# Marked neighbours turned by transposing transfers instead of TensorE, in a LoRA, cross-attention and graph-network kernel

## The chip, the cores and the metric

The kernel runs on one NeuronCore of a Trainium2 chip. The metric is the device time of one execution in microseconds, the median over runs. Below, TensorE is PE in the profile's lines, VectorE is DVE, ScalarE is ACT, GpSimd is POOL, SyncE is SP. SP computes nothing here; it waits for semaphores and issues DMA transfers, one after the other, in its own order.

## The reference

Four batches (b = 0 to 3) of 256 rows of 512 numbers pass through four layers. The context has 4 x 64 rows of 512.

```
x   = x + 0.5 * sum_n softmax(x @ router_W.T + router_b)[n] * (a_sum @ lora_B[n].T)   # 8 experts, rank 64
      # a_sum = x times the sum of the context's rows taken as lora_A; then nan_to_num
Q,K,V = x@Wq.T+bq, ctx@Wk.T+bk, ctx@Wv.T+bv         # 32 heads of 16, 64 keys with a mask
x   = layernorm(x + softmax(Q K.T / 4) V @ Wo.T + bo) * g + b
for layer in (L2, L3):                              # two graph layers, the same weights
    idx = the 8 nearest of 512 points by ctx (64 coordinates)       # per batch
    for i in range(4):
        p = leaky_relu(x)
        x = x + (W[i] @ p + sum over the 8 neighbours of W[i] @ p[neighbour]) / 9
```

As the weights of centre and neighbour are the same, the sum is a product with a 512x512 matrix per batch: the 0/1 matrix of neighbours, turned so that the contracted index lies on the partitions, plus the identity. That matrix is what this change is about.

## The kernel before, in words

The work is cut into steps named by kind, batch and part, as dist1_3. Five texts (PE_STEPS, ACT_STEPS, DVE_STEPS, POOL_STEPS, SP_STEPS, lines 47 to 123) list the steps of each engine in the order in which it runs them; a number behind a colon is the PSUM bank (PE) or the buffer (DVE) used. An engine works strictly in its order; each step first waits for the semaphores of what it reads and of what still reads the place it writes. A step of TensorE that takes a bank waits until the bank's former content has been read (wait_read, line 575). The orders come out of a search outside the kernel; nothing of its costs stands in the code. Products are made of two float32r parts (hi, lo) in three passes.

Steps that this text speaks of:

- Loads: SP issues all first loads before its step list, in the order xyz0, ctxT, x0, loraB, wk, xyz1, x1, small, wq, wv (with bv and mask_col), wo (with g_all and b_all) (line 490). ld_x2, ld_xyz2 and so on come later.
- lora, router (PE), low, rE (ACT), rA, rB (DVE): the router's softmax, and mix, the rows weighted for each expert. mixed (PE) turns them, mh and ml make hi and lo. ua, ub, uc (PE, 24 + 12 + 12 products) are the update; raw and nan (DVE) make x1 of it. xh, xl split x1; qa, qb, qc (PE, 24 + 12 + 12 products) are the queries; qh, qf (ACT), ql (POOL) keep them as q_hi and q_lo.
- keys and values (PE), kh, kl, vr. kst writes the keys to DRAM, ks (six transfers) brings them back as k_stack. qsh (eight transfers) and qs (four) bring q_hi and q_lo into q_stack, sd (two) the shifts. sc (PE) gives scores for the maxima (mx), shift turns these, w (PE) is the stacked product that the softmax reads, at and norm attend, rows and oa, ob, oc are the output product, st, ce, ln the layer norm.
- dist (PE, line 676) gives the distances of 128 points to all 512 in one bank. near (DVE, line 1157) takes the 8 greatest (max) and writes the tile with these replaced by -2^127 into near_of[:, i] in bf16. There is one near_of for all batches, so near of batch b waits until batch b-1 has been turned.
- adjT (PE, line 677): when all four near of a batch are there, 16 transposes of 128x128 bf16 with ident_h turn near_of into two PSUM banks. adjC (ACT, line 867) makes the 0/1 matrix adj[:, b] of it in one 128x2048 instruction, reading PSUM. diag (POOL, line 1095) adds the identity. adj[:, 2] and adj[:, 3] hold att_hi and wo_hi before, so adjC2 and adjC3 wait for the last oc.
- Graph layers: units b, i = 0 to 7. wa, wb, wc, wd (PE) multiply with W, uh, ul split, ga, gb, gc, gd (PE) multiply with adj[:, b], pt (DVE) adds to points, lk (DVE), ph (ACT), pl (POOL) make the next p. The units of batch 0 start while the attention of later batches still runs.

points[:, b] is used for other things early: it holds the coordinates of batch 1, the bias bv (until vr), and x_bo[b], the input turned with bo added (ACT, xb, line 899).

The step that the change takes off TensorE:

```python
for m in range(KC):
    for n in range(KC):
        last = pe.transpose(dst[:, m * H + n * P:m * H + (n + 1) * P],
                            near_of[:, n, m * P:(m + 1) * P], ident_h[:])
last.then_inc(turned_done, 1)
```

## Time and profile before

| | |
|---|---|
| median of 3 runs | 377.6 us (377.03 to 379.24) |
| the profiled execution | 378.0 us from its first to its last instruction |
| TensorE busy | 367.6 us, 97% |
| VectorE busy | 272.0 us, 72% |
| ScalarE busy | 177.0 us, 47% |
| GpSimd busy | 129.0 us, 34% |
| mean granted TensorE clock | 0.995 |

The profile is of one execution. An engine's busy time counts its instructions, not its waits or its issues of transfers. For TensorE, matmuls overlap each other by modelled ends, so differences between starts tell its pace. The last instruction of a transfer's issue (SPq) is the time that SP is held by it; the landing comes later. "The chain" is followed back from the last instruction to what released each.

### The profile page before, as it was taken

What the parts mean: (1) busy time and instruction counts of PE and PEld (TensorE: products, weight loads), DVE (VectorE), ACT (ScalarE), POOL (GpSimd) and SP (SyncE); (2) the same over time, 40 slices, a digit from 0 to 9 for tenths busy, and PEclk for the clock granted to TensorE, in tenths of its full rate; (3) what the DMA queues carried; (4) which work ended last, traced back from release to release, by engine and by line L of the source; (5) the groups of instructions that cost most, each with busy time, mean ns of one, the idle gap of its engine ahead of it and who ended that gap; (6) DMA issues with size and microseconds to landing.
All of it is one profiled execution on the core that took longest, in us unless ns stands there. A gap on an engine that the chain in (4) does not pass through costs nothing.

```text
span 378.0 us, 6569 instructions
## 1 busy us (share of the span) xinstructions
PE 367.6 (97%) x2396; PEld 311.0 (82%) x2396; DVE 272.0 (72%) x427; ACT 177.0 (47%) x308; POOL 129.0 (34%) x125
## 2 busy tenths in 40 slices
...
GB/s 201 317 348 159 24 55 155 78 9 178 34 20 232 105 0 116 102 0 3 0 3 2 0 0 2 0 2 1 2 0 2 0 2 0 3 0 2 0 85 139
DMA packets 25056, 22.47 MB, mean 59 GB/s; under 512 B 9537, under 2 KB 20546, under 8 KB 25026
## 3 DMA queue, kind: packets, MB, share of 16 engines
...
q10 hardware_dynamic: 674, 0.02, 0.1%
...
## 4 chain that ended last, share of the span: by engine, by line
PE 85%; DVE 4%; ACT 4%; DMA 3%; issue 2%; SPq 1%; DVEq 0%; ACTq 0%
PE slot L564 82%; DMA wk<-in_WkT 3%; ACT k_blk_hi L943 2%; PE slot L684 1%; PE slot L693 1%; SPq L448 1%; PE slot L725 1%; ACT probT L976 1%; DVE p_full L1321 1%; DVE points L1331 1%; ACT adj L874 1%; DVE inv_full L1267 0%; ACT L976 0%; DVE stats L1282 0%; DVE shift L1255 0%
## 5 line engine op out<-in xcount | busy, mean ns | idle before, releaser
L1065 POOL TENSOR_TENSOR p_lo<-p_full,p_hi 128x512 fp32r<-128x512 f32 x64 | 86.0, 1362 | 157.1 <-ACT p_hi L1016 157.0
L1026 ACT ACTIVATE u_hi<-slot 128x512 fp32r<-128x512 f32 x64 | 36.2, 593 | 69.3 <-PE slot L564 69.0
L1326 DVE TENSOR_TENSOR u_lo<-slot,u_hi 128x512 fp32r<-128x512 f32 x64 | 42.4, 684 | 31.5 <-ACT u_hi L1026 31.5
L1016 ACT ACTIVATE p_hi<-p_full 128x512 fp32r<-128x512 f32 x64 | 39.0, 627 | 55.3 <-DVE p_full L1321 55.3
L564 PE MATMUL slot<-adj,u_hi 128*128 128x512 f32 x256 | 64.8, 392 | 0.1
L564 PE MATMUL slot<-fs_hi,p_hi 128*128 128x256 f32 x256 | 64.8, 286 | 0.0
L1331 DVE SCALAR_TENSOR_TENSOR points<-slot,points 128x512 f32<-128x512 f32 x64 | 42.7, 684 | 30.4 <-PE slot L564 30.4
L564 PE MATMUL slot<-adj,u_lo 128*128 128x512 f32 x256 | 64.1, 391 | 0.0
L564 PE MATMUL slot<-fs_lo,p_hi 128*128 128x256 f32 x256 | 64.1, 283 | 0.0
L1321 DVE SCALAR_TENSOR_TENSOR p_full<-points 128x512 f32<-128x512 f32 x64 | 54.3, 863 | 8.9 <-POOL p_lo L1065 6.3
L564 PEld LDWEIGHTS slot<-adj,u_lo 128*128 128x128 f32 x256 | 47.5, 188 | 10.1 <-issue 0.4
L564 PEld LDWEIGHTS slot<-adj,u_hi 128*128 128x128 f32 x256 | 46.4, 188 | 8.8 <-DVE u_lo L1326 0.3
L564 PEld LDWEIGHTS slot<-fs_hi,p_hi 128*128 128x128 f32 x256 | 48.9, 191 | 1.6 <-issue 0.7
L564 PEld LDWEIGHTS slot<-fs_lo,p_hi 128*128 128x128 f32 x256 | 49.0, 191 | 0.9 <-issue 0.2
L564 PE MATMUL slot<-fs_hi,p_lo 128*128 128x256 f32 x256 | 42.9, 285 | 0.1
L564 PEld LDWEIGHTS slot<-fs_hi,p_lo 128*128 128x128 f32 x256 | 36.6, 191 | 1.8 <-issue 0.8
L1065 POOL TENSOR_TENSOR q_lo<-q_full,q_hi 128x512 fp32r<-128x512 f32 x8 | 10.7, 1348 | 46.5 <-ACT q_full L930 46.5
L976 ACT ACTIVATE probT<-slot,mask_col 128x1024 f32<-128x1024 f32 x16 | 17.7, 1116 | 16.2 <-PE slot L564 16.0
L1255 DVE TENSOR_REDUCE shift<-slot 128x16 f32<-128x1024 f32 x16 | 19.4, 1218 | 1.5 <-PE slot L564 1.5
L943 ACT ACTIVATE k_blk_hi<-kT_hi,half_col 32x256 fp32r<-32x256 f32 x32 | 14.4, 497 | 0.9 <-PE slot L564 0.5
L564 PE MATMUL slot<-xyz_n,xyz 128*128 128x512 f32 x24 | 13.9, 685 | 0.3 <-issue 0.3
L564 PE MATMUL slot<-mixT_hi,loraB_hi 128*128 128x256 f32 x64 | 13.7, 296 | 0.0
...
## 6 DMA issues: line engine op xcount, KB each, us to landing
q_stack<-q_hi SPq DMA_DIRECT2D x32, 128.0 KB, 2.5
x_in<-in_xT SPq DMA_DIRECT2D x8, 256.0 KB, 4.2
q_stack<-q_lo SPq DMA_DIRECT2D x16, 128.0 KB, 2.4
out_points<-points SPq DMA_DIRECT2D x8, 256.0 KB, 2.0
...
```

Of the source, the lines that this page charges most:

```text
L448: sp.dma_start(dst, src).then_inc(loads[name], 16)
L564: return pe.matmul(dst, lhsT, rhs, start=start, stop=stop, skip_group_check=True)
L684: last = pe.transpose(dst[:, m * H + n * P:m * H + (n + 1) * P], near_of[:, n, m * P:(m + 1) * P], ident_h[:])
L943: act.activation(k_blk_hi[rows, :, 2 * j + a, :], kT_hi[rows, :, b * V:(b + 1) * V].bitcast(F32), ACT.Copy, scale=half_col[rows, a:a + 1]) ...
L976: act.activation(probT[:, i % 2, :], both_banks("w", b, i)[:], ACT.Exp, bias=mask_col[:, b:b + 1], scale=QK_SCALE).then_inc(prob_ready, 1)
L1016: act.activation(p_hi[b][:, (i % 2) * H:(i % 2 + 1) * H], p_full[:, p_buf[b, i]], ACT.Copy)\
L1026: act.activation(half_of(u_hi[:, u], i % 2), bank("wa", b, i // 2, i % 2), ACT.Copy)\
L1065: pool.tensor_tensor(lo[:, cut], full[:, cut], hi[:, cut].bitcast(F32), ALU.subtract)\
L1255: dve.tensor_reduce(pairs, both_banks("sc", b, i)[:].rearrange("p (j a v) -> p j a v", a=2, v=V), AX_X, ALU.max, negate=True).then_inc(max ...
L1321: dve.scalar_tensor_tensor(p_full[:, p_buf[b, i]], pts, SLOPE, pts, ALU.mult, ALU.max)\
L1326: dve.tensor_tensor(half_of(u_lo[:, u], i % 2), bank("wa", b, i // 2, i % 2), half_of(u_hi[:, u], i % 2).bitcast(F32), ALU.subtract).then_ ...
L1331: dve.scalar_tensor_tensor(pts, bank("ga", b, i // 2, i % 2), 1.0 / (TOPK + 1), pts, ALU.mult, ALU.add).then_inc(points_ready, 1)
```

## The change

Each of the four near of a batch is followed by its own transfer nt (SP): a transposing DMA that writes near_of[:, i], 128x512 in bf16, turned into nearT[b][:, :, i*128:(i+1)*128] in SBUF. Sixteen of them take the place of the four adjT with their 64 transposes. nearT lies in points[:, 0] for batch 0, in points[:, 2] for batch 1 (nt1 waits until vr has read bv there), and for batches 2 and 3 in near_late, which lies where q_stack lies (nt2 and nt3 wait for the last w). near of batch b waits for all four transfers of batch b-1, adjC for those of b. adjC reads nearT in place of PSUM. xb0 waits for adjC0 and xb2 for adjC1, as they write the same places. ident_h and its two instructions on POOL go. All five orders are new; kst stands later in SP's, behind qsh0.

In the diff, the texts of the orders are cut to their first lines.

```diff
 PE_STEPS = """
-mb0:0 dist0_0:7 dist0_1:5 lora0:6 dist0_2:2 dist0_3:4 router0:0 keys:6,7 lora1:2 mixed0:0,1 router1:2 values:4,5
-mixed1:2,0 dist1_0:7 adjT0:4,5 ua0:3,6 ub0 uc0 dist1_1:4 dist1_2:5 ua1:1,2 qa0:7,3 qb0 dist1_3:6 ub1 sc0_0:4,5 qc0
-uc1 sc0_1:0,1 lora2:6 adjT1:2,3 router2:0 dist2_0:1 sc0_2:4,5 sc0_3:6,7 qa1:3,2 dist2_1:7 qb1 dist2_2:4 shift0:5
-dist2_3:1 lora3:6 mixed2:0,3 router3:5 sc1_0:6,7 qc1 ua2:0,4 w0_0:2,3 sc1_1:6,7 ub2 sc1_2:2,3 w0_1:6,7 uc2 w0_2:2,3
-w0_3:6,7 at0_0:0,1,5 at0_1 at0_2 at0_3 sc1_3:6,7 qa2:3,2 qb2 shift1:0 mixed3:6,7 norm0:4,5 qc2 sc2_0:0,1 rows0:5,4
...
+dist0_0:4 dist0_2:7 lora0:3 router0:1 dist0_1:5 dist0_3:0 mixed0:6,4 mb0:2 lora1:1 dist1_0:0 dist1_1:3 dist1_2:1
+ua0:6,5 ub0 router1:2 uc0 keys:6,7 dist1_3:4 mixed1:0,5 values:2,3 qa0:1,4 qb0 ua1:6,0 sc0_2:2,3 ub1 qc0 uc1 lora2:7
+sc0_0:0,1 qa1:6,5 router2:7 sc0_1:2,3 sc0_3:0,1 qb1 qc1 mixed2:7,2 dist2_1:3 shift0:4 ua2:0,1 sc1_2:2,3 sc1_0:4,5
+ub2 sc1_1:2,3 w0_1:6,7 w0_0:4,5 lora3:0 uc2 w0_2:6,7 at0_0:2,3,0 at0_1 w0_3:4,5 router3:1 sc1_3:6,7 at0_2 at0_3
+shift1:5 dist2_2:6 qa2:4,7 qb2 mixed3:3,5 norm0:0,1 dist2_0:2 qc2 ua3:6,1 sc2_2:4,5 sc2_0:2,3 ub3 uc3 dist2_3:7
+w1_1:4,5 rows0:0,1 w1_0:2,3 oa0 w1_2:2,3 at1_0:6,7,4 at1_1 ob0 w1_3:2,3 oc0 at1_2 at1_3 sc2_1:2,3 qa3:0,1 norm1:4,5
+sc2_3:6,7 qb3 rows1:4,3 qc3 oa1 ob1 shift2:2 oc1 wa0_0:7,6,1 sc3_1:0,1 wb0_0 wc0_0 sc3_2:4,5 sc3_0:2,3 wd0_0
+ga0_0:0,1 w2_0:4,5 gb0_0 gc0_0 w2_1:6,7 w2_2:4,5 at2_0:2,3,0 at2_1 w2_3:6,7 gd0_0 at2_2 at2_3 wa0_1:4,1,1 wb0_1
+wc0_1 rows2:5,3 norm2:6,7 wa1_0:0,2,0 wd0_1 wb1_0 wc1_0 wd1_0 sc3_3:6,7 oa2 shift3:6 ob2 ga1_0:6,7 oc2 gb1_0
...
 ACT_STEPS = """
-sq0 low0 rE0 lbh wqh low1 mh0_0 rE1 mh0_1 kh kb0 sq1 woh mh1_0 adjC0 xh0_0 mh1_1 xh0_1 sq2 qh0_0 xb0_0 qf0_0 qh0_1
-xb0_1 qf0_1 xh1_0 low2 adjC1 xh1_1 rE2 kb1 qh1_0 sh0 qf1_0 xb1_1 low3 mh2_0 mh2_1 vb0 qh1_1 qf1_1 rE3 xb1_0 ex0_0
...
+sq0 low0 rE0 lbh mh0_0 sq1 mh0_1 low1 adjC0 rE1 wqh xh0_0 kh kb0 xh0_1 mh1_0 mh1_1 xb0_1 woh qf0_0 xb0_0 qh0_0 sq2
+qh0_1 qf0_1 xh1_0 vb0 low2 xb1_0 xh1_1 rE2 kb1 mh2_0 qf1_0 sh0 qf1_1 mh2_1 qh1_0 qh1_1 adjC1 ex0_0 ex0_1 xb1_1 low3
+ex0_2 ex0_3 xh2_0 xh2_1 rE3 sh1 kb2 ac0_0 ac0_1 vb1 qf2_0 mh3_1 mh3_0 qh2_0 ah0_1 xb2_1 xb2_0 qh2_1 ah0_0 qf2_1
...
 DVE_STEPS = """
-mr fa a_ready fm init near0_0 rA0 near0_1 near0_3 near0_2 rB0 rA1 mk ml0_0 rB1 kl vr ml0_1 near1_0 ml1_0 raw0_0
-nan0_0 raw0_1 xl0_0 nan0_1 ml1_1 xl0_1 near1_1 near1_2 near1_3 raw1_0 mx0_0 nan1_0 raw1_1 mx0_1 xl1_0 nan1_1 rA2
-mx0_3 xl1_1 mx0_2 near2_0 rB2 near2_1 sl0 near2_2 ml2_0 mx1_0 ml2_1 rA3 near2_3 rB3 mx1_1 raw2_0 mx1_2 nan2_0 raw2_1
...
+a_ready near0_0 near0_2 rA0 rB0 mr near0_3 init near0_1 ml0_0 fa ml0_1 fm raw0_0 near1_0 near1_1 rA1 raw0_1 nan0_0
+rB1 near1_2 kl nan0_1 xl0_0 near1_3 xl0_1 vr ml1_0 ml1_1 mx0_2 mk raw1_0 nan1_0 raw1_1 xl1_0 nan1_1 mx0_0 xl1_1 rA2
+mx0_1 rB2 mx0_3 ml2_0 near2_1 sl0 ml2_1 mx1_2 mx1_0 raw2_0 mx1_1 nan2_0 raw2_1 nan2_1 mx1_3 rA3 xl2_0 xl2_1 rB3 sl1
+rc0 near2_2 dv0_1 ml3_0 dv0_0 ml3_1 near2_0 al0_0 mx2_0 mx2_2 raw3_1 al0_1 raw3_0 near2_3 nan3_0 nan3_1 xl3_1 st0_0
...
 POOL_STEPS = """
-zb wql lbl zk wol ql0_0 ql0_1 zr ql1_0 ql1_1 ql2_0 ql2_1 diag0 diag1 pl0_0 pl0_1 ql3_0 ql3_1 pl1_1 pl1_0 pl0_2 pl0_3
...
+lbl zb zr wql zk ql0_0 ql0_1 wol ql1_1 ql1_0 ql2_1 ql2_0 pl0_0 diag0 pl0_1 pl0_2 diag1 ql3_1 pl0_3 ql3_0 pl1_0 pl1_1
...
 SP_STEPS = """
-kst ld_xyz2 ks0 ld_x2 qsh0 qs0 ld_x3 sd0 qsh1 qs1 ks1 sd1 ld_fs qsh2 qs2 sd2 ks2 ld_xyz3 qsh3 sd3 ks3 qs3
+nt0_1 nt0_0 nt0_2 nt0_3 ld_xyz2 nt1_2 nt1_3 ld_x2 qsh0 kst nt1_0 nt1_1 qs0 ks0 sd0 ld_x3 qsh1 sd1 qs1 ks1 ld_fs ks2
+qsh2 qs2 sd2 ld_xyz3 qsh3 ks3 qs3 sd3 nt2_3 nt2_2 nt2_0 nt2_1 nt3_0 nt3_2 nt3_1 nt3_3
 """
@@ -152,7 +153,7 @@
             banks_of[kind, b, i] = where
             read_before[kind, b, i] = list(dict.fromkeys(holder[k] for k in where if k in holder))
         for part, k in enumerate(where):
-            holder[k] = (kind, b, i, 0 if kind in ("keys", "values", "adjT", "sc", "w") else part)
+            holder[k] = (kind, b, i, 0 if kind in ("keys", "values", "sc", "w") else part)
     for kind, b, i, where in dve_steps:
         if kind == "lk":
             p_buf[b, i], p_holder[b, i] = where[0], holder.get(("p", where[0]))
@@ -174,7 +175,6 @@
         points = sb("points", [P, B, ST, H])
         adj = sb("adj", [P, B, KC, H], F32R)
         ident = sb("ident", [P, P])
-        ident_h = sb("ident_h", [P, P], BF16)
         xyz_0 = sb("xyz", [P, H])
         xyz_n0 = sb("xyz_n", [P, H])
         near_of = sb("near_of", [P, KC, H], BF16)
@@ -194,6 +194,7 @@
         v_rows = sb("v_rows", [P, B // 2, H])
         v_blk = sb("v_blk", [P, NH // 2, PART])
         wk, wv = under(("wk", [P, KC, H], F32), ("wv", [P, KC, H], F32))
+        near_late, = under(("near_late", [P, 4, H], F32))
         q_stack = sb("q_stack", [P, NH // 2, S], F32R)
         ctx_t, = under(("ctx_t", [P, KC, B * V], F32))
         attT, = under(("attT", [P, KC, S], F32))
@@ -240,6 +241,9 @@
         x_bo = [points[:, b].rearrange("p t h -> p (t h)").rearrange("p (c s) -> p c s", c=KC) for b in range(B)]
+        nearT = [place.rearrange("p a n -> p (a n)").bitcast(BF16)[:, 0:KC * H].rearrange("p (m n) -> p m n", m=KC)
+                 for place in (points[:, 0], points[:, 2], near_late[:, 0:2], near_late[:, 2:4])]
+
         front = ExitStack()
         def fb(name, shape, dt=F32):
@@ -523,6 +527,14 @@
                             row = PART * part + HD * a
                             src = k_bounce[which].rearrange("c (j a d) b v -> b a d (c j) v", a=2, d=HD)[b, a]
                             sp.dma_start(k_stack[row:row + HD, :, a, :].bitcast(F32), src).then_inc(k_stacked, 16)
+                elif kind == "nt":
+
+                    if b == 1:
+                        sp.wait_ge(v_ready, 1)
+                    if b >= 2:
+                        after(sp, weights_done, "w", B - 1, KC - 1)
+                    after(sp, near_ready, "near", b, i)
+                    sp.dma_start_transpose(nearT[b][:, :, i * P:(i + 1) * P], near_of[:, i]).then_inc(turned_done, 16)
                 elif kind == "qsh":
                     after(sp, q_hi_ready, "qh", b, 0, each=2)
                     after(sp, q_hi_ready, "qh", b, 1, each=2)
@@ -593,8 +605,6 @@
                     pe.wait_ge(ctx_filled, 1)
                 elif kind == "dist":
                     after(pe, near_ready, "near", b, i)
-                elif kind == "adjT":
-                    after(pe, adj_copied, "adjC", b)
                 elif kind == "sc":
                     after(pe, max_ready, "mx", b, i)
                 elif kind == "shift":
@@ -674,16 +684,6 @@
                     after(pe, sq_ready, "sq", b)
                     pe.wait_ge(dve_consts, 2)
                     mm(bank("dist", b, i), xyz[b][:, i * P:(i + 1) * P], xyz_n[b], True, True).then_inc(dist_done, 1)
-                elif kind == "adjT":
-                    pe.wait_ge(idents, 2)
-                    for n in range(KC):
-                        after(pe, near_ready, "near", b, n)
-                    dst = both_banks("adjT", b)[:].bitcast(BF16)
-                    for m in range(KC):
-                        for n in range(KC):
-                            last = pe.transpose(dst[:, m * H + n * P:m * H + (n + 1) * P],
-                                                near_of[:, n, m * P:(m + 1) * P], ident_h[:])
-                    last.then_inc(turned_done, 1)
                 elif kind == "mixed":
                     after(pe, mix_ready, "rB", b, each=ST)
                     cols = cols_of("mixed", b)
@@ -868,11 +868,11 @@
                     if b >= 2:
                         after(act, output_done, "oc", B - 1)
-                    after(act, turned_done, "adjT", b)
+                    act.wait_ge(turned_done, 16 * KC * (b + 1))
                     act.wait_ge(dve_consts, 3)
                     act.activation(adj[:, b].rearrange("p m n -> p (m n)"),
-                                   both_banks("adjT", b)[:].bitcast(BF16), ACT.Relu,
+                                   nearT[b].rearrange("p m n -> p (m n)"), ACT.Relu,
                                    bias=taken_bias[:], scale=TAKEN_SCALE).then_inc(adj_copied, 1)
                 elif kind == "low":
                     if b >= 1:
@@ -900,10 +900,12 @@
                     loaded(act, "bo_col")
                     after(act, x1_ready, "nan", b, i)
+                    if b == 0:
+                        after(act, adj_copied, "adjC", 0)
                     if b == 1:
                         after(act, dist_done, "dist", 1, 3)
                     if b == 2:
-                        act.wait_ge(v_ready, 1)
+                        after(act, adj_copied, "adjC", 1)
                     for c in (2 * i, 2 * i + 1):
                         act.activation(x_bo[b][:, c], x1[:, c, :], ACT.Identity, bias=bo_col[:, c:c + 1])\
                            .then_inc(x_bo_ready, 1)
@@ -1033,9 +1035,6 @@
             link(pool.memset(ident[:], 0.0))
             pool.affine_select(out=ident[:], in_=ident[:], compare_op=ALU.not_equal, fill=1.0, base=0,
                                pattern=[[-1, P]], channel_multiplier=1).then_inc(idents, 1)
-            link(pool.memset(ident_h[:], 0.0))
-            pool.affine_select(out=ident_h[:], in_=ident_h[:], compare_op=ALU.not_equal, fill=1.0, base=0,
-                               pattern=[[-1, P]], channel_multiplier=1).then_inc(idents, 1)
             link(pool.memset(diag[:], 1.0))
             link(pool.affine_select(out=diag[:], in_=diag[:], compare_op=ALU.is_ge, fill=0.0, base=0,
@@ -1055,7 +1054,7 @@
                     last = pool.memset(cols[:, :, 2 * c + half], 1.0)
             last.then_inc(blk_consts, 1)
             pool.wait_ge(blk_consts, 2)
-            pool.wait_ge(idents, 2)
+            pool.wait_ge(idents, 1)
             def low_part(lo, full, hi, parts, ready):
@@ -1158,7 +1157,7 @@
                     after(dve, dist_done, "dist", b, i)
                     if b >= 1:
-                        after(dve, turned_done, "adjT", b - 1)
+                        dve.wait_ge(turned_done, 16 * KC * b)
                     tile = bank("dist", b, i)
                     link(dve.max(top8[:, i], tile))
                     dve.match_replace(near_of[:, i], top8[:, i], tile, TAKEN).then_inc(near_ready, 1)
```

## Rows read from the trace of the kernel before

**Rows 1.** The page: its span, busy times, and the chain's shares
```profile
span 378.0 us, 6569 instructions
...
PE 367.6 (97%) x2396; PEld 311.0 (82%) x2396; DVE 272.0 (72%) x427; ACT 177.0 (47%) x308; POOL 129.0 (34%) x125
...
PE 85%; DVE 4%; ACT 4%; DMA 3%; issue 2%; SPq 1%; DVEq 0%; ACTq 0%
```

**Rows 2.** Windows: from:to, length, busy us by engine, granted clock, DMA share, GB/s
```profile
37.00:375.00 338.00, 334.94 (x2275) 289.80 (x2274) 250.37 (x379) 160.95 (x282) 111.65 (x90) 1.00 0.14 36
...
15.90:20.20 4.30, 4.30 (x13) 3.55 (x14) 3.98 (x10) 0.53 (x1) 0.00 (x0) 0.65 1.10 335
```

**Rows 3.** Chain in order of time: start, us, what
```profile
4.29 11.36 DMA wk<-in_WkT
...
36.15 0.89 PE slot L684 x16
...
59.58 0.91 PE slot L684 x16
...
175.80 0.91 PE slot L684 x16
...
219.75 0.91 PE slot L684 x16
```

**Rows 4.** Timeline, ScalarE: start, us, instruction, idle time before
```profile
40.50 1.97 ACT L874 ACTIVATE adj<-slot,taken_bias 128x2048 fp32r<-128x2048 bf16 x1
...
201.12 1.98 ACT L874 ACTIVATE adj<-slot,taken_bias 128x2048 fp32r<-128x2048 bf16 x1 [4.17 <-PE slot L564]
```

**Rows 5.** Timeline of SP: its issues
```profile
12.37 2.82 SPq L448 DMA_DIRECT2D wv<-in_WvT  x1
...
19.48 0.43 SPq L448 DMA_DIRECT2D b_all<-in_ln_b  x1
...
35.26 0.83 SPq L525 DMA_DIRECT2D k_stack<-k_hi_bounce  x2
...
56.96 5.29 SPq L496 DMA_DIRECT2D q_stack<-q_hi  x8
...
89.41 2.52 SPq L496 DMA_DIRECT2D q_stack<-q_lo  x4
```

**Rows 6.** DMA issues: KB each, us from issue to landing
```profile
q_stack<-q_hi SPq DMA_DIRECT2D x32, 128.0 KB, 2.5
...
b_all<-in_ln_b SPq DMA_DIRECT2D x1, 256.0 KB, 9.0
```

**Rows 7.** Timeline, VectorE: steps near0, nan0_0 and the following raw0_1
```profile
15.42 0.69 DVE L1163 MAX8 top<-slot 128x8 f32<-128x512 f32 x1
...
16.82 0.69 DVE L1163 MAX8 top<-slot 128x8 f32<-128x512 f32 x1
...
42.17 0.43 DVE L1237 TENSOR_SCALAR scratch<-x_in 128x512 f32<-128x512 f32 x1
...
44.44 0.68 DVE L1225 SCALAR_TENSOR_TENSOR x_in<-slot,x_in 128x512 f32<-128x512 f32 x1
```

**Rows 8.** Timeline, TensorE: keys, values, mixed1, dist1_0, transposes, two products of the update
```profile
15.89 8.83 PE L564 MATMUL slot<-ctx_m,wk 128*128 128x256 f32 x32 [2.43 <-DMA wk<-in_WkT]
...
27.32 7.10 PE L564 MATMUL slot<-wv,ctx_t 128*128 128x512 f32 x16
34.26 1.04 PE L693 MATMUL slot<-ident,mix 128*128 128x128 f32 x8
35.13 1.02 PE L564 MATMUL slot<-points 128*128 128x512 f32 x2
35.99 1.06 PE L684 MATMUL slot<-ident_h,near_of 128*128 128x128 bf16 x16
...
37.17 0.40 PE L564 MATMUL slot<-mixT_hi,loraB_lo 128*128 128x256 f32 x2
37.41 0.40 PE L564 MATMUL slot<-mixT_lo,loraB_hi 128*128 128x256 f32 x2
```

More of the change, by code:

```diff
@@ new lines @@
+w3_0:0,1 gc1_0 w3_1:2,3 gd1_0 ga0_1:4,0 w3_2:2,3 at3_0:6,7,1 at3_1 gb0_1 w3_3:2,3 gc0_1 gd0_1 at3_2 at3_3 dist3_2:2
+wa1_1:5,3,1 wb1_1 wc1_1 dist3_0:6 norm3:0,1 wd1_1 wa0_2:4,7,0 ga1_1:0,2 gb1_1 dist3_1:1 gc1_1 gd1_1 wb0_2 wc0_2
+dist3_3:2 wd0_2 rows3:5,3 oa3 ob3 oc3 ga0_2:4,7 gb0_2 gc0_2 wa2_0:0,2,0 wb2_0 wa1_2:3,5,1 wc2_0 gd0_2 wd2_0 wb1_2
+ga2_0:7,1 gb2_0 wc1_2 wd1_2 gc2_0 gd2_0 ga1_2:6,4 wa3_0:2,0,0 wb3_0 gb1_2 wc3_0 gc1_2 gd1_2 wd3_0 wa0_3:6,7,1 wb0_3
+wc0_3 ga3_0:4,5 wd0_3 gb3_0 wa1_3:1,0,0 gc3_0 gd3_0 wb1_3 wc1_3 wd1_3 ga0_3:5,6 ga1_3:4,3 gb1_3 wa3_1:2,7,0 gc1_3
```

93 lines of the change are left out of this document (41 added, 52 removed).

## The prediction

> **What bounds the kernel now.** I read the page first: TensorE is busy 97% of a span of 378.0 us, the next engine (VectorE) 72%, and the chain that ended last runs 85% through TensorE [rows 1]. The windows say the same by stage: from 37 to 375 us TensorE is busy 334.94 of 338.00 us, so it sits idle 3.06 us in all, at a granted clock of 1.00 [rows 2]. In that stretch a microsecond of TensorE work taken out is a microsecond gained, and one added wait of TensorE is one lost. The chain in order of time then shows what the removed step costs: the four groups of 16 transposes (L684) stand on it with 0.89, 0.91, 0.91 and 0.91 us, and before all of them the chain hangs on the load of wk, which lands at 15.65 us [rows 3]. So there are two regimes: before about 16 us the loads set the pace, after it TensorE does.
>
> The profiled execution took 378.0 us, 0.4 us more than the median of the three timed runs (377.6). The sum is made against 378.0, and 0.4 us is taken off at the end. A measurement of this kernel can tell about 0.5% (1.9 us) from no change.
>
> **Removed.** The 64 transposes: 0.89 + 3 x 0.91 = 3.62 us of the chain [rows 3]. TensorE's PSUM banks 4,5 and 2,3 are no longer held by them; what that gives is left to the new orders. POOL loses one memset and one select of ident_h before 2.2 us, with 16 us idle before its next work: nothing. ScalarE's adjC reads SBUF in place of PSUM; it takes 1.97 us for 128x2048 [rows 4], the shape stays, and a few tenths more or less would be hidden on an engine that is busy half of the span: nothing.
>
> **Added.** Sixteen transposing transfers of 128 KB, SBUF to SBUF, all issued by SP. The trace has none. What I need is how long SP is held by one (i), and when the first four have landed (T). From below: a plain 128 KB transfer q_stack<-q_hi holds SP 5.29/8 = 0.66 us and lands 2.5 us after its issue [rows 5, 6]. From above: the longest time any issue held SP is 2.82 us (wv) [rows 5]. It can't be below nothing, since SP has no such transfer now. I take i between 0.7 and 1.0 us, near the row of the same size and the same memories, and keep 2.8 us for the range.
>
> The Trainium skill speaks on both sides here. *Advanced Engine Details and Errata*, section X-Bar Transpose (TRN2), says that transposing DMAs are as fast as regular ones; by it i is the lower bound and the sum stays as below. *VectorE: DVE Perf Modes*, section The three transpose paths, gives 1309 ns for one 128x128 bf16 transpose by DMA against 390 ns on TensorE; if four of them in a transfer simply add up, i is an estimated 5.2 us, and the change ends near 393 us. On TensorE's side that page does not fit this case: 16 transposes take 0.91 us in the stream here, 57 ns each [rows 3].
>
> **First set (b = 0), the place that I think decides.** near0 needs until about 18.5 us (two of its steps of 1.40 us each [rows 7] stand behind rB0, which can't start before x0 has been through lora0 and router0), but SP is issuing the initial loads until 19.48 + 0.43 = 19.9 us, and its queue is full: b_all, issued at 19.48, lands 9.0 us later, at 28.5 us [rows 5, 6]. Packets of the SP queue land in order, so nt0 comes behind b_all: 28.5 us plus 0.5 MB at the 380 GB/s the queue then reaches, 1.4 us: T = 29.9 us.
>
> In DVE's new order near1_0 comes right after raw0_0, and it now waits for all four of nt0 (near_of is single). Behind it on DVE queue near1_0 and near1_1 (1.40 us each, from start to start), rA1 (0.3 us), raw0_1 (0.7) with nan0_0 (from the start of nan to the next raw 2.3) and rB1 (1.8) [rows 7]. On ScalarE adjC0 waits for the same four, with rE1, wqh and xh0_0 behind it; adjC0's 1.97 us lie beside the two near steps, so rE1 is in time for rB1. TensorE's mixed1 needs rB1: it can start at M = T + 8.0 = 37.9 us.
>
> When would TensorE be there by itself? x1 lands about 2.1 us after wk (0.75 MB), near 18 us. From there the new order has half of lora1 (0.9), dist1_0 to dist1_2 (2.6), 48 products of the update at 0.12 us (5.8), router1 (0.1), the keys (6.9: 8.7 us from start to start now, of which the low clock takes 1.5 to 1.8) and dist1_3 (0.9): 35.2 us [rows 8]. So mixed1 waits about 2.7 us. Against before: at 35.99 us, where the first transposes start, TensorE has done the values (6.9) and mixed1 (0.9), which the new order has still before it, while at M the new one has done three more dist (2.6) and the 48 update products (5.8) [rows 8]. That is 0.5 us more, so the orders are even for M = 36.5 us. With M = 37.9 the new one is 1.4 us behind. After M the values (6.9 us) cover near1_2, kl, nan0_1, xl0_0 and near1_3 (7.4 us with mixed1's 0.9 in front), and wq_lo is ready at T + 10.6: nothing more is lost.
>
> **The clock.** From 15.9 to 20.2 us the granted clock is 0.65 on average, after TensorE had sat idle from 13.5 to 15.9 us [rows 2, 8]; at 1.00 the same work would take 1.5 us less. The new order has idle time just before 18 us too (only mixed0 and mb0 are left until x1 is there), so I count the same loss in both, and keep 1.5 us to either side for the range.
>
> **Second set (b = 1).** nt1_2 and nt1_3 wait for v_ready (about 47 us) and stand ahead of ld_x2; lora2 comes at 57.6 us (the first product of the queries at M + 7.8 = 45.7, then 96 products of 0.12 us and one score step, 11.9 us in all), and x2 needs 3 us plus 2i: hidden up to i = 3. On SP then: 8 issues of q_hi (5.3 us from 57.1 us on, when q_hi is whole), kst (0.8), nt1_0 and nt1_1 (2i), 4 of q_lo (2.5), 6 of k_stack (2.8), 2 of shiftT (1.4, at q_hi's rate), and 2.5 us to the last landing: 72.4 + 2i [rows 5, 6]. TensorE reaches w0_1 after 84 more products (10.1), six score steps (2.8) and 3.8 us of lora2, mixed2, dist2_1, shift0 and router2, at 57.6 + 16.7 = 74.3 us. It is covered up to i = 0.95, all but the end of my interval; above it TensorE loses 2 us for each us of i. I take 0.
>
> **Third and fourth (b = 2, 3).** nt2 waits for the last scores' product w3_3 (170 us now), adjC2 ran at 201 us [rows 4]; near3 waits for nt2, and adjC3 ran some 20 us later. SP has nothing else to do there. Even 4 x 2.8 + 2.5 = 14 us is hidden: nothing.
>
> **The orders.** Everything else is the same work in another order. With 3.06 us idle left in 37 to 375 us [rows 2] it can't win more than that there; I count 0, with up to 2 us either way.
>
> **Sum.** 378.0 - 3.62 + 1.4 = 375.8 us; less 0.4: 375.4 us.
>
> **Rivals.** (A) *The front is not late.* For it: the wait on DVE hangs on a queue whose rate I estimated, and a T of 28.5 would give M = 36.5 (loss 0). With 1 to 2 us of the 3.06 idle us recovered it gives 372 to 374 us. Against: nt0 can hardly land before b_all.
> (B) *The gain is absorbed.* nt0 lands 2 to 3 us later than I think (a transposing packet that takes twice as long as a plain one puts T at 31.3), or i is 1.5 us, which costs 1 us at w0: 377.3 to 380 us.
> (C) *The transfers hold SP, and it is slower.* One mechanism: i. With i = 2.8 the last of nt0 is issued at 31.1 and lands at 33.6, M = 41.6, a loss of 5.1 us in place of 1.4; before w0_1 another 2 x (2.8 - 0.95) = 3.7 us. Total 375.4 + 3.7 + 3.7 = 382.8 us. For it: k_stack's transfers of 64 KB hold SP 0.42 us, b_all's of 256 KB 0.43 and q_hi's of 128 KB 0.66 [rows 5], so the issue cost goes by the form and not by the bytes, and a transpose is a new form; wv's issue shows how long one can be held. The turning point: with T = 19.9 + 4i + 2.5, the loss (4i - 6.1) + 2(i - 0.95) exceeds 3.62 from i = 1.9 us on.
> (D) *The change doesn't do what it says:* TensorE's work shrinks by 3.6 us, but it idles as much more in the order as searched. It would give 378 us and is counted with B.
>
> **Numbers.** Forecast 0.40 (374 to 377.3), A 0.20 (371 to 374), B with D 0.17 (377.3 to 380), C 0.23 (380 and up, open end). The range 371.5 to 381 leaves out 0.02 of A and 0.18 of C. Faster by over 0.5% means below 375.7: A (0.20) and 0.28 of the forecast's 0.40, in sum 0.48. Slower means above 379.5: C and 0.02 of B, 0.25. The same: 0.27.
>
> **What would show it.** No L684 in the new trace and TensorE's busy time lower by about 3.6 us. On SP, sixteen new issues with their length: under 1 us for the forecast, over 1.9 for C. On DVE, an idle gap before a near1 step at 28 to 30 us released by the DMA of nearT, and on TensorE a gap of 2 to 3 us before the transposes of mixed1 (none for A, over 6 us for C). No gap before the first q_stack,k_stack product. It would be wrong if nt0 lands ahead of the loads issued before it, if transposing transfers slow the other transfers, or if the new order opens gaps elsewhere in 45 to 375 us that have nothing to do with the transfers.

## The result, and the profile after

The changed kernel takes 391.0 us (389.54 to 392.31, 4 runs) against 377.4 us before (377.6 in the table ahead, with one run fewer); the ratio is 1.035 (95% interval 1.0318 to 1.0389). It is slower by 13.6 us, outside the range of the prediction and on the other side of its forecast. The profiled execution took 389.54 us, its span 387.7 us.

First the page of the kernel after, the lines that answer to [rows 1]:

```profile
span 387.7 us, 6449 instructions
...
PE 367.5 (95%) x2332; PEld 307.1 (79%) x2332; DVE 277.0 (71%) x427; ACT 172.4 (44%) x304; POOL 130.8 (34%) x123
...
PE 70%; DVE 15%; SPq 6%; issue 4%; ACT 2%; DMA 1%; POOL 1%; DVEq 0%; ACTq 0%; POOLq 0%
```

The transposes are gone, yet TensorE is as busy as before (367.5 against 367.6 us), and it is idle for 387.7 - 367.5 = 20.2 us against 378.0 - 367.6 = 10.4. So two things have to be found: about 10 us of new idle time, and what filled up the 3.6 us that were taken out. The chain says where to look: VectorE has 15% of it in place of 4%, and SP's issues 6% in place of 1% [rows 1].

Windows of the kernel after (columns as in [rows 2]): the stretch of [rows 2], then three short ones around the largest stall.

```profile
37.00:375.00 338.00, 326.44 (x2157) 277.27 (x2156) 249.55 (x370) 160.21 (x288) 116.62 (x86) 0.99 0.18 41
```

```profile
66.30:69.90 3.60, 0.19 (x2) 0.02 (x1) 3.57 (x4) 0.63 (x1) 1.83 (x2) 0.94 1.01 314
69.90:72.90 3.00, 3.00 (x12) 2.81 (x13) 2.90 (x8) 2.13 (x6) 0.00 (x0) 0.51 0.74 158
72.90:76.00 3.10, 3.10 (x26) 2.86 (x26) 1.84 (x4) 2.53 (x7) 0.00 (x0) 1.00 0.74 165
```

From 37 to 375 us TensorE is now idle 11.56 us in place of 3.06. Behind the stall at 66 us it runs at a granted clock of 0.51, the level of 1.2 GHz, for some 3 us: pairs of 128x256 matmuls start 0.43 us apart there (from 71.32 us on) and 0.24 us apart right after (from 72.95 us on). This is TensorE's timeline at the new waits (in brackets: idle time before, and what ended it):

```profile
39.37 1.06 PE L693 MATMUL slot<-ident,mix 128*128 128x128 f32 x8 [1.65 <-DVE mix L1213]
48.06 0.48 PE L576 MATMUL slot<-x_hi,wq_hi 128*128 128x256 f32 x2 [0.77 <-DVE near_of L1163]
...
69.88 1.22 PE L576 MATMUL slot<-k_blk_hi,q_hi 128*128 128x512 f32 x2 [3.41 <-DVE shift L1254]
...
151.43 0.36 PE L576 MATMUL slot<-fs_hi,p_hi 128*128 128x256 f32 x1 [1.39 <-issue]
```

The first is the wait for nt0 that the prediction worked out. The largest has no transfer in it. VectorE and GpSimd of the kernel after, in front of it (the steps nan1_1 and mx0_0, and wol):

```profile
62.38 1.51 DVE L1236 TENSOR_SCALAR scratch<-x_in 128x512 f32<-128x512 f32 x1
63.92 1.67 DVE L1237 SCALAR_TENSOR_TENSOR x<-x_in,scratch 128x512 f32<-128x512 f32 x1
65.62 1.39 DVE L1238 TENSOR_SCALAR scratch<-x_in 128x512 uint32<-128x512 f32 x1
67.05 1.67 DVE L1239 COPY_PREDICATED x<-scratch,x_in 128x512 f32<-128x512 uint32 x1
68.62 1.21 DVE L1254 TENSOR_REDUCE shift<-slot 128x16 f32<-128x1024 f32 x1
```

```profile
61.87 6.26 POOL L1064 TENSOR_TENSOR wo_lo<-wo_raw,adj 128x512 fp32r<-128x512 f32 x4
```

The same step nan1_1 in the kernel before, its first two instructions:

```profile
60.43 0.58 DVE L1237 TENSOR_SCALAR scratch<-x_in 128x512 f32<-128x512 f32 x1
61.04 0.69 DVE L1238 SCALAR_TENSOR_TENSOR x<-x_in,scratch 128x512 f32<-128x512 f32 x1
```

These four instructions of nan1_1 took 0.58, 0.69, 0.45 and 0.75 us before (the first of nan0_0 took 0.43 [rows 7]). Here they take 6.2 us in sum instead of 2.5, and for nearly all that time GpSimd does wol, which the new order puts there. The reduction that TensorE waits for (L1254) is queued behind them.

SP of the kernel after; L537 is the transposing transfer:

```profile
19.24 8.50 SPq L537 DMA_TRANSPOSE points<-near_of  x4
...
49.72 2.50 SPq L537 DMA_TRANSPOSE points<-near_of  x2
52.31 1.51 SPq L452 DMA_DIRECT2D x_in<-in_xT  x2
...
66.63 3.75 SPq L537 DMA_TRANSPOSE points<-near_of  x2
```

One transfer holds SP 2.1 us while its queue is full of loads, 1.25 us with little else in flight and 1.9 us behind the q_hi transfers; single ones took 1.19 to 2.64. The forecast took 0.7 to 1.0. The table of DMA issues has them from issue to landing (median us), early and late ones:

```profile
points<-near_of SPq DMA_TRANSPOSE x8, 4.9
near_late<-near_of SPq DMA_TRANSPOSE x8, 2.5
```

### The profile page after: what moved, and what is told of

Same layout as the page of the kernel before. It is cut to its first block, busy times and chain, and to the rows that moved or that the text cites. A ratio compares the mean times of both kernels' runs of the same rounds, so it can differ in the third digit from the quotient of the medians.

```text
span 387.7 us, 6449 instructions
## 1 busy us (share of the span) xinstructions
PE 367.5 (95%) x2332; PEld 307.1 (79%) x2332; DVE 277.0 (71%) x427; ACT 172.4 (44%) x304; POOL 130.8 (34%) x123
## 4 chain that ended last, share of the span: by engine, by line
PE 70%; DVE 15%; SPq 6%; issue 4%; ACT 2%; DMA 1%; POOL 1%; DVEq 0%; ACTq 0%; POOLq 0%
PE slot L576 68%; SPq L452 4%; DVE p_full L1320 2%; DVE points L1301 2%; SPq L537 2%; DVE points L1330 2%; DMA points<-near_of 1%; DVE near_of L1163 1%; DVE top L1162 1%; DVE x L1237 1%; DVE scratch L1238 1%; ACT k_blk_hi L945 1%; DVE u_lo L1325 1%; DVE scratch L1236 1%; PE slot L693 1%
## 5 line engine op out<-in xcount | busy, mean ns | idle before, releaser
L576 PE MATMUL slot<-adj,u_hi 128*128 128x512 f32 x256 | 65.9, 394 | 2.2 <-ACT u_hi L1028 1.6
L576 PE MATMUL slot<-adj,u_lo 128*128 128x512 f32 x256 | 66.6, 394 | 0.9 <-DVE u_lo L1325 0.9
L576 PEld LDWEIGHTS slot<-adj,u_lo 128*128 128x128 f32 x256 | 46.3, 188 | 10.1 <-DVE u_lo L1325 1.5
L576 PE MATMUL slot<-fs_hi,p_lo 128*128 128x256 f32 x256 | 43.9, 285 | 0.3 <-ACT p_hi L1018 0.3
L576 PEld LDWEIGHTS slot<-fs_hi,p_lo 128*128 128x128 f32 x256 | 38.2, 191 | 3.9 <-issue 1.0
L1254 DVE TENSOR_REDUCE shift<-slot 128x16 f32<-128x1024 f32 x16 | 19.4, 1220 | 8.2 <-PE slot L576 8.2
L576 PE MATMUL slot<-x_hi,wq_hi 128*128 128x256 f32 x64 | 14.3, 307 | 1.0 <-DVE near_of L1163 0.8
L945 ACT ACTIVATE k_blk_hi<-kT_hi,half_col 32x256 fp32r<-32x256 f32 x32 | 14.4, 497 | 0.4
```

Source lines behind the costliest of these rows:

```text
L576: return pe.matmul(dst, lhsT, rhs, start=start, stop=stop, skip_group_check=True)
L945: act.activation(k_blk_hi[rows, :, 2 * j + a, :], kT_hi[rows, :, b * V:(b + 1) * V].bitcast(F32), ACT.Copy, scale=half_col[rows, a:a + 1]) ...
L1254: dve.tensor_reduce(pairs, both_banks("sc", b, i)[:].rearrange("p (j a v) -> p j a v", a=2, v=V), AX_X, ALU.max, negate=True).then_inc(max ...
```

## Experiments

All are built from the kernel after. "Theory O" in the expectations is that the new orders make the loss, "theory T" that the transfers do. Medians are of runs taken beside runs of the kernel before (377.2 to 377.8 us each time).

### The two halves of the change, apart

e1_old_orders: the five orders of before, without adjT, with the 16 transfers in SP's. From the kernel after it differs in the orders alone.

```diff
 PE_STEPS, ACT_STEPS, DVE_STEPS, POOL_STEPS: those of before, without adjT0 to adjT3
 SP_STEPS
-kst ld_xyz2 ks0 ld_x2 qsh0 qs0 ...
+nt0_0 nt0_1 nt0_3 nt0_2 kst ld_xyz2 ks0 nt1_0 ld_x2 nt1_1 nt1_2 nt1_3 qsh0 qs0 ...
```

> The five orders of before, with adjT taken out and the sixteen transfers put into SP's order (nt0 first, nt1 around ld_x2 and ahead of qsh0, nt2 and nt3 last). If the loss comes from the new orders (theory O), this is faster than before by the 3.6 us of the transposes: 373 to 375 us. If it comes from the transfers themselves (theory T: SP held, VectorE waiting for landings, packets in the way of others), it is slower than before: 380 us or more.

Measured: 377.3 us (10 runs), ratio 0.9988 (0.9963 to 1.0014): the whole loss is gone, but the gain of 3.6 us that theory O expected isn't there either. Its page:

```profile
span 373.9 us, 6454 instructions
...
PE 362.9 (97%) x2332; PEld 306.8 (82%) x2332; DVE 272.4 (73%) x427; ACT 177.2 (47%) x308; POOL 127.7 (34%) x123
```

e7_no_transfers: the new orders without any transfer (near writes where adjC reads), with adjC1 right behind sq2. An earlier form, e2_no_transfers, had left adjC1 in its place, and near2_1 waited for it.

```diff
-                    sp.dma_start_transpose(nearT[b][:, :, i * P:(i + 1) * P], near_of[:, i])...
-                    act.wait_ge(turned_done, 16 * KC * (b + 1))
+                    after(act, near_ready, "near", b, 0) ... 3
-dve.match_replace(near_of[:, i], ...)
+dve.match_replace(near_at[b][:, i], ...)
```

> The new orders with no transfers at all: near writes the marked tile where adjC reads it, unturned, so the neighbours' matrix is left unturned (that part of the computation is left out). Theory O: little is won, 2 to 4 us, as the wait before mixed1 (1.8 us) goes: 386 to 389 us. Theory T: the whole loss goes, 378 us or less.

> The new orders with no transfers, as in the kernel without transfers above, and adjC1 moved to behind sq2 on ScalarE, so that near2_1 no longer waits for it (an artefact of that kernel, 5 us; the turning is left out again). Theory O: 386 to 388 us, as most of the loss has nothing to do with the transfers. Theory T: 380 us or less.

Measured: e2 394.0 us (1.0399 to 1.0493), e7 388.2 us, ratio 1.027 (1.0247 to 1.0298). Both leave the matrix of neighbours unturned. TensorE and GpSimd of e7_no_transfers have the largest stall of the kernel after, at the same step and of the same length, without any transfer:

```profile
65.91 1.22 PE L576 MATMUL slot<-k_blk_hi,q_hi 128*128 128x512 f32 x2 [3.42 <-DVE shift L1256]
...
57.90 6.26 POOL L1065 TENSOR_TENSOR wo_lo<-wo_raw,adj 128x512 fp32r<-128x512 f32 x4
```

e4_plain_copy kept the transfers as plain copies (again unturned; each row of a partition goes in four pieces of 256 bytes):

```diff
-sp.dma_start_transpose(nearT[b][:, :, i * P:(i + 1) * P], near_of[:, i])
+sp.dma_start(nearT[b][:, :, i * P:(i + 1) * P], near_of[:, i].rearrange("p (m n) -> p m n", m=KC))
```

> The changed kernel with each transposing transfer made a plain copy of the same 128 KB between the same places (the turning is left out). Theory T with the form of the transfer as its cause: issues fall from 1.2 to 2.6 us to 0.6 us each and 5 us or more are won. Theory O: the wait before mixed1 shrinks by 1 to 2 us and little else, 388 to 390 us.

Measured: 391.3 us (1.0315 to 1.0425). With SP's queue full at 20 us four plain copies hold it 6.90 us; four transposing ones 8.50. For the last two batches, with nothing else in flight, one plain copy holds it 0.60 us in the median, one transposing transfer 1.22.

What follows: the transfers in the old orders are as fast as the transposes. With the same transfers the new orders are 391.0 - 377.3 = 13.7 us slower than the old ones. With neither transfers nor transposes they are still 10.8 us slower than the kernel before, which has 3.6 us of transposes more to do. In the change the transfers account for 391.0 - 388.2 = 2.8 us; the rest is the orders. e8_old_tuned put dist2_0 ahead of router2 on TensorE in e1, where it waited 0.62 us:

> The old orders with the transfers and dist2_0 ahead of router2 on TensorE. The transposes used to fill the time in which ScalarE makes low2 (a gap of 0.8 us at 56 us with the transfers); dist2_0 fills it now: 0.5 to 0.8 us faster than the old orders with the transfers, 376.5 us, and 1 us faster than before. If removed work is given back elsewhere: the same as before.

Measured: 377.1 us (12 runs, 0.9966 to 1.0013), no difference, where 1 us had been expected.

### The waits of the new orders, one by one

e3_wol_early moves wol on GpSimd, away from nan1_1 (the expectation calls the step nan1_0).

```diff
-lbl zb zr wql zk ql0_0 ql0_1 wol ql1_1 ...
+lbl zb zr wql zk wol ql0_0 ql0_1 ql1_1 ...
```

> The changed kernel with one step moved: GpSimd's wol before ql0_0, so that its four subtractions no longer run beside VectorE's nan1_0. Theory O in its sharpest form (GpSimd's tensor_tensor doubles the time of VectorE's steps out of SBUF, and TensorE waits 3.6 us for the maxima queued behind): 3 to 4 us faster than the changed kernel, 387 to 388 us. Theory T: no change, 391 us.

Measured: 393.6 us (1.039 to 1.047). The four instructions were back at 0.42, 0.69, 0.43 and 0.76 us and TensorE's wait was gone, but nothing was won: the median is 2.6 us above the kernel after. The next row of TensorE's timeline in e3_wol_early shows why:

```profile
82.50 1.77 PE L576 MATMUL slot<-q_stack,k_stack 100*128 100x256 f32 x7 [4.14 <-DMA q_stack<-shiftT]
```

A second wait, for q_stack at w0, ran beside the first and had been hidden by it; alone it is 0.7 us longer than the first was. The other 2 us of the difference are not explained. On SP, nt1_0 and nt1_1 (3.77 us), q_lo and k_stack stood ahead of shiftT. This is the wait that the prediction priced at 2(i - 0.95), and I had overlooked it when I wrote the expectation. e5_sp_early adds an SP order with both earlier; e6_front_too adds four small moves before 60 us.

```diff
 SP_STEPS
-nt0_1 nt0_0 nt0_2 nt0_3 ld_xyz2 nt1_2 nt1_3 ld_x2 qsh0 kst nt1_0 nt1_1 qs0 ks0 sd0 ...
+nt0_1 nt0_0 nt0_2 nt0_3 ld_xyz2 kst ks0 nt1_0 nt1_1 nt1_2 nt1_3 ld_x2 qsh0 qs0 sd0 ...
```

> The changed kernel with wol before ql0_0 on GpSimd, and SP's order changed: kst and ks0 right after ld_xyz2, and all four nt1 ahead of ld_x2. Theory O (two delays lay side by side, VectorE beside GpSimd's wol and SP's queue before w0_1, so that taking away the first alone showed the second): both stalls near 66 to 82 us go, 4 to 5 us, and the stretch at half clock after them, 1.7 us: 385 us. If the losses of this stretch have another cause, it stays at 390 to 394 us.

> The kernel before this one with three more steps moved: mb0 and mr back to the front of TensorE's and VectorE's orders, near1_3 right behind near1_2, and xl0_0 ahead of nan0_1. Theory O: mb0 costs 1 us less (it fills the wait for the coordinates) and the 0.9 us wait before the first queries goes: 1.5 to 2 us faster than with SP's order alone. No change if those waits are hidden by the landing of nt0.

Measured: e5 387.2 us (1.022 to 1.0282), 2 us above what was expected, e6 386.7 us (1.0203 to 1.026), no clear difference from e5 where 1.5 to 2 us were expected. Now mixed1 was the largest wait, as VectorE's and TensorE's timelines of e5_sp_early show:

```profile
32.08 0.70 DVE L1162 MAX8 top<-slot 128x8 f32<-128x512 f32 x1 [5.25 <-DMA points<-near_of]
```

```profile
39.98 1.51 PE L693 MATMUL slot<-ident,mix 128*128 128x128 f32 x8 [4.51 <-DVE mix L1213]
```

VectorE stands still for 5.25 us with rA1 and rB1 queued behind near1_0. e11_router_first puts them ahead:

```diff
 ACT_STEPS
-low1 adjC0 rE1 wqh
+low1 rE1 adjC0 wqh
 DVE_STEPS
-raw0_0 near1_0 near1_1 rA1 raw0_1 nan0_0 rB1 near1_2
+raw0_0 rA1 raw0_1 nan0_0 rB1 near1_0 near1_1 near1_2
```

> e5_sp_early with rA1, raw0_1, nan0_0 and rB1 ahead of near1_0 on VectorE (near1_0 waits for the landing of nt0, and mixed1 of TensorE hung on rB1 behind it), and rE1 ahead of adjC0 on ScalarE. Theory E: TensorE's wait of 4.7 us at 35 us goes, and the stretch of 3.41 us at half clock behind it (1.7 us): 387.2 - 6.4 = 381 us (380 to 383). Rival (the wait covers another one close behind it, as in e3_wol_early): a wait for near1 or the values' consumers takes its place and it stays above 385 us.

Measured: 385.0 us (1.0145 to 1.0244). The wait at 35 us went, but only 2.2 us of the 6.4 came out; TensorE then waited 1.58 us for near1_3, and a slow clock stretch appeared at 146.7 us. e13_pool_early takes GpSimd away from VectorE in that late stretch:

```diff
-pl0_0 diag0 pl0_1 pl0_2 diag1 ql3_1 pl0_3 ql3_0
+pl0_0 diag0 pl0_1 diag1 ql3_1 pl0_2 pl0_3 ql3_0
```

> e11_router_first with diag1 and ql3_1 of GpSimd (adj<-adj,ident and q_lo<-q_full,q_hi) moved ahead of pl0_2, into its idle time from 131.5 to 139.1 us. In e11_router_first they ran at 140.35 and 142.05 us beside VectorE's points<-points,rstd,b_all (2.48 us for two, elsewhere 1.42) and p_full<-points (3.27 us for two, elsewhere 1.28), and TensorE then waited 1.6 us for p_hi, with a stretch of 3.41 us at half clock behind it (1.7 us). Theory C (VectorE is slowed by GpSimd's tensor_tensor beside it, and that makes the wait): p_full goes back to 1.3 to 2 us, the wait of 1.6 us goes, 385.0 - 3.3 = 381.7 us (381 to 383.5). Rival (the slow VectorE instructions have another reason, or the wait is ScalarE's): p_full stays at 3.27 us wherever GpSimd is, and the time within 1 us of 385.0.

VectorE and GpSimd of e11_router_first, then of e13_pool_early, at the same steps:

```profile
138.46 2.48 DVE L1301 SCALAR_TENSOR_TENSOR points<-points,rstd,b_all 128x512 f32<-128x512 f32 x2
141.05 3.27 DVE L1320 SCALAR_TENSOR_TENSOR p_full<-points 128x512 f32<-128x512 f32 x2
...
139.11 1.28 POOL L1064 TENSOR_TENSOR p_lo<-p_full,p_hi 128x512 fp32r<-128x512 f32 x1 [7.59 <-ACT p_hi L1018]
140.35 1.74 POOL L1097 TENSOR_TENSOR adj<-adj,ident 128x512 fp32r<-128x512 f32 x1
142.05 1.72 POOL L1064 TENSOR_TENSOR q_lo<-q_full,q_hi 128x512 fp32r<-128x512 f32 x1
```

```profile
140.20 2.47 DVE L1301 SCALAR_TENSOR_TENSOR points<-points,rstd,b_all 128x512 f32<-128x512 f32 x2
142.78 1.29 DVE L1320 SCALAR_TENSOR_TENSOR p_full<-points 128x512 f32<-128x512 f32 x2
...
140.84 1.28 POOL L1064 TENSOR_TENSOR p_lo<-p_full,p_hi 128x512 fp32r<-128x512 f32 x1 [5.06 <-ACT p_hi L1018]
```

Measured: 382.9 us (1.0085 to 1.017), 2.1 us less; the runs of the two kernels don't overlap (382.0 to 383.2 against 383.6 to 386.0). The same two p_full take 1.29 us instead of 3.27 once GpSimd is idle beside them, while points<-points,rstd,b_all, which still has p_lo beside it, stays at 2.47. GpSimd's own instructions got shorter too (1.74 and 1.72 us back to 1.31 and 1.30). That VectorE and GpSimd slow each other is shown by this pair, and by e3_wol_early. The windows of the same stretch (e11_router_first, then e13_pool_early) show that the low clock went with the wait:

```profile
146.80:150.00 3.20, 3.20 (x17) 3.20 (x17) 2.47 (x3) 2.42 (x6) 3.12 (x3) 0.50 0.63 143
```

```profile
146.80:150.00 3.20, 3.03 (x26) 2.69 (x26) 2.38 (x4) 2.17 (x5) 3.12 (x3) 1.00 0.80 184
```

e14_front_too then moves three steps:

```diff
 PE_STEPS: mb0 ahead of dist0_0
 DVE_STEPS: mr ahead of a_ready, near1_3 right behind near1_2
```

> e13_pool_early with near1_3 right behind near1_2 and mr ahead of a_ready on VectorE, and mb0 ahead of dist0_0 on TensorE. Theory E (single waits in the order, each worth its own length once nothing lies beside it): TensorE's wait of 1.74 us at 43.9 us for near1_3 goes, and up to 1 us before 10 us: 1.7 to 2.7 us below e13_pool_early, 379.5 us (378.5 to 381). Rival (each wait that is taken away is replaced by the next): no more than 0.7 us below e13_pool_early.

Measured: 380.4 us (1.0049 to 1.0096), 2.5 us less. The same three moves were in e6_front_too, where TensorE still waited 4.55 us for mixed1 and they gave no clear gain.

### SP's queue once more

e15_two_more moves two more steps, and e16_x2_first mends what it broke:

```diff
 e15_two_more, against e14_front_too
-DVE: near1_3 kl nan0_1 xl0_0 xl0_1 vr       ACT: dev3 ph3_0 uh2_0 uh2_1
+DVE: near1_3 nan0_1 xl0_0 xl0_1 kl vr       ACT: dev3 uh2_0 uh2_1 ph3_0
 e16_x2_first, against e15_two_more
-SP:  ld_xyz2 kst ks0 nt1_0 nt1_1 nt1_2 nt1_3 ld_x2 qsh0
+SP:  ld_xyz2 ld_x2 kst ks0 nt1_0 nt1_1 nt1_2 nt1_3 qsh0
```

> e14_front_too with two steps moved: kl of VectorE behind xl0_1, and ph3_0 of ScalarE behind uh2_1. In e14_front_too TensorE waits 1.78 us at 42.7 us for x_lo (kl, 1.65 us, runs on VectorE ahead of nan0_1), and 1.57 us at 199.4 us for u_hi, which on ScalarE is queued behind ph3_0 (it waits 5.98 us for a p_full that VectorE gives late, after 3.39 us for points<-points,rstd,b_all beside GpSimd). Theory E (each wait was put there by the order and is worth its own length): both go, 380.4 - 1.5 - 1.6 = 377.3 us (376.5 to 378.5), as before. Rival (the two waits hide others of the same length): over 379 us.

> e15_two_more with ld_x2 ahead of kst on SP and nothing else. In e15_two_more the later kl held up kst (46.46 us), and ks0 and the four transposing transfers nt1 (5.12 us of SP from 52.85 us on) stood ahead of ld_x2, which was issued at 58.07 us; TensorE waited 4.78 us for it (until 61.49 us), with a stretch of 3.41 us at half clock behind it. Theory S (SP's queue made that wait): it goes, 386.8 - 4.8 - 1.7 = 380.3 us (379 to 381). Rival (another wait stands behind it, for q_stack or the shifts at w0): over 382.5 us.

Measured: e15 386.8 us (1.0225 to 1.0279), 9 us over the expectation; e16 379.9 us (1.0035 to 1.0081). SP and TensorE of e15_two_more, then SP of e16_x2_first:

```profile
46.46 0.38 SPq L515 DMA_DIRECT2D k_lo_bounce<-kT_lo  x1
...
52.85 5.12 SPq L536 DMA_TRANSPOSE points<-near_of  x4
58.07 1.04 SPq L451 DMA_DIRECT2D x_in<-in_xT  x2
```

```profile
61.49 3.48 PE L575 MATMUL slot<-x_in,points 128*72 128x256 f32 x8 [4.78 <-DMA x_in<-in_xT]
```

```profile
42.62 0.91 SPq L451 DMA_DIRECT2D x_in<-in_xT  x2
...
53.04 5.13 SPq L536 DMA_TRANSPOSE points<-near_of  x4
```

A VectorE step, kl, put 7.3 us later (44.78 us in place of 37.46) held up the store of the keys, which held up k_stack and four transposing transfers, which held up a load that had nothing to do with them. With the load in front, 6.8 us came back. Of e15's own two moves, the wait at 42 us shrank from 1.78 to 1.53 us only (nan0_1 now ran beside wq_lo on GpSimd, and its second instruction took 1.64 us for 0.69).

### Halves of the orders joined, a miss

e9_old_early runs the old orders to about 100 us and the new ones after; e10_old_late is its mirror; e12_both is e11_router_first before the joint and the old orders after it.

```diff
 e9_old_early: old PE to sc2_2, ACT to ex1_0, DVE to ce0_1, POOL to ql2_1, SP to sd1; then the new, without the steps done
 e10_old_late, e12_both: new PE to dist2_3, ACT to qf2_1, DVE to raw3_0, POOL to ql2_0, SP to ks1; then the old
```

> All 16 transfers. The orders of before (as in e1_old_orders) up to about 100 us on every engine (TensorE through sc2_2), and the rest in the new orders. It says where the loss of the new orders sits. Theory E (it is mostly an early loss: waits of TensorE before 105 us, with the half clock behind them): the stalls of TensorE from 110 us on are 2.9 us more in e5_sp_early than in e8_old_tuned, so this run is 377.3 + 3 = 380 us (379 to 382). Rival L (the late orders are what is slow, through VectorE beside GpSimd from 140 us on): over 383 us.

> The mirror of e9_old_early: the new orders of e5_sp_early up to about 105 us (TensorE through dist2_3), the rest in the orders of before. Theory E: it keeps the early loss, 387.2 - 3 = 384 us (382.5 to 386), with the wait of 4.7 us of TensorE for mixed1 at 35 us and a stretch of half clock behind it. Rival L: 380 us or less. If early and late losses add up, e9 + e10 = e1 + e5 = 764.5 us.

> e11_router_first up to about 105 us and the orders of before after it. Theory E: 381 - 3 = 378 us (376.5 to 380), no faster than the orders of before from the start. Rival L: 375 us or less.

Measured: 389.6, 389.3 and 386.9 us (1.0272 to 1.0347, 1.0271 to 1.0367, 1.021 to 1.0299). Neither theory fits both e9 and e10, and each run with the old orders in one half is slower than e1, which has them in both. TensorE of e9_old_early, then of e10_old_late, right behind the joint:

```profile
103.19 0.51 PE L575 MATMUL slot<-mixT_hi,loraB_hi 128*128 128x256 f32 x2 [1.93 <-DVE shift L1253]
...
116.27 0.74 PE L575 MATMUL slot<-q_stack,k_stack 100*128 100x256 f32 x4 [1.72 <-ACT probT L977]
```

```profile
119.43 1.02 PE L575 MATMUL slot<-q_stack,k_stack 100*128 100x256 f32 x4 [4.54 <-DVE shift L1253]
```

The joint makes waits of its own, so these runs don't divide the loss into early and late.

## Why the prediction was wrong

**The step that failed is "The orders. Everything else is the same work in another order ... I count 0, with up to 2 us either way".** The term measured 13.7 us: e1 and the kernel after differ in the orders alone (377.3 and 391.0 us). e7 says the same from the other side: it has the new orders, no transposes and no transfers, should be 3.6 us faster than before and is 10.8 slower, 14.4 us in all; with 2.8 for the transfers, -3.6 + 14.4 + 2.8 gives the 13.6 us that were lost.

I had bounded what a new order can win by the idle time that was left, 3.06 us [rows 2], and took "up to 2 us" for what it can lose from no row at all. That has no such bound. In the kernel before no single wait of TensorE behind 37 us is over 0.8 us; an order that is wrong in several places waits in each. Rival D had this mechanism (TensorE idles in the order as searched), but only as far as 378 us, and the last sign of being wrong, gaps that have nothing to do with the transfers, is the one that came.

The GpSimd order alone would have told of two of them: it puts 6 us of wol beside nan1_1, and diag1 and ql3_1 beside p_full. Mending them took 391.0 us to 387.2 (wol, SP's order), 385.0 (router ahead of near1), 382.9 (GpSimd away from p_full), 380.4 (three early steps) and 379.9 (ph3_0, kl, ld_x2). The last 2.5 us to before stay unexplained in detail; in e16_x2_first TensorE still waits 1.36 us at 43 us, 1.25 at 15 us and 0.6 to 0.9 us each at 199, 291 and 326 us.

**Removed: right as TensorE's work, not as time.** e1 shows it by itself: PE 362.9 us busy for 367.6, that is 4.7 less, of which 3.62 was forecast; the rest lies within the 1.7 us that the stretch of low clock near 17 us cost the profiled execution of before [rows 2], and which this run didn't have. In the kernel after the 3.6 us were filled up again, in part by the low clock: a stretch of 3.41 us behind the stall at 66 us costs 1.7 us. The rest of it is open. The prediction also set the 378.0 us of the profiled execution, a span, beside the median time; time lies 1.7 us above the span, so that execution was 2 us slower than the median and not 0.4. Its low clock near 17 us goes with that; 9 of the 13 runs of before beside e1 have a mean granted clock of 1.000 and a median of 377.1 us, the others 0.995 and 379.3.

**Added, i: mis-sized.** 0.7 to 1.0 us was taken from the row nearest in size; it is 1.2 to 2.6 us. The upper bound of 2.8 held. (At i = 5.2 us the prediction's own formula gives 397 us, not the 393 that it names.) The rule of the Trainium skill (*Advanced Engine Details and Errata*, X-Bar Transpose (TRN2)) that transposing DMAs are as fast as regular ones fits the time of the kernel, which stays the same with plain copies (e4), and the landing (2.5 us, as q_hi's [rows 6]), but not the issue: in the same place, with nothing else in flight, a transposing transfer held SP 1.22 us and the plain copy of e4 0.60. The 1309 ns per 128x128 block of the Trainium skill (*VectorE: DVE Perf Modes*, The three transpose paths) do not add up here: a whole 128x512 transfer, four blocks, had landed 2.5 us after its issue.

**First set: right as a mechanism.** The first transfer of nt0 landed at 28.3 us, behind b_all (27.9), as assumed. The last landed at 31.35 us for 29.9, VectorE resumed at 31.45, and mixed1 started at 39.37 us, which is T + 8.0 as worked out. TensorE idled 1.65 us there, 2.7 forecast; that these are near each other is luck, as nt0 was 1.45 us late and TensorE itself got there at 37.7 us, not at 35.2. Rival C described this and the wait at w0_1; by after against e7 the two are worth 2.8 us, a fifth of what was lost, so C names a real mechanism and not the one that decided. **Second set:** the wait at w0_1 exists (4.14 us in e3_wol_early) but lay beside the one at 66 us in the kernel after. **Third and fourth:** right, no wait of TensorE or VectorE there ends with a DMA.

**The gain where the orders stay.** e1 loses no time, and gains none. Over its 10 runs the span is 374.3 us in the median against 376.0 before: 1.7 us of the 3.6 come out, the rest turned into waits of under 0.8 us each. And the time around the span grew: 1.70 to 1.79 us in all 13 runs of before beside it, but 2.00 to 2.05 us in four runs and 2.9 to 3.3 us in six of e1. What that is stays open.
